# Expert additions written straight into an output with spare rows, and statistics, roots, counting products and gate waits moved

## The chip, the cores and the metric

The kernel runs on one core of a Trainium2 chip. The metric is the device time of one execution in microseconds (us), the median of three runs. For each version one further execution is recorded by the hardware profiler, and all rows below come from that one. The engines are TensorE (PE in the rows: matmuls, and PEld: its weight loads), VectorE (DVE), ScalarE (ACT) and GpSimd (POOL); SP only issues DMAs, and ACT and POOL issue some too. "SPq", "ACTq" are those engines issuing a DMA.

## The reference, cut to what matters

Two sequences of 1024 tokens, 256 features, all in fp32. Three sublayers, each added to the stream `x` after a layernorm:

```python
x = x + attn(layernorm(x))          # linear attention: q,k,v projections, elu+1, two decayed
                                    # running sums over time, normalised, times w_out
x = x + xattn(layernorm(x), ctx)    # 16 heads over 154 context rows:
    att = softmax(where(mask, -inf, (q @ k.T) / 8 * side))
    out = (att @ v) @ Wo + bo
x = x + ffn(layernorm(x))           # 8 experts, 2 per token, and a shared expert
    scores = softmax(x @ gate_w.T);  idx = top_k(scores + gate_b, 2)
    y = sum over the two chosen experts of score * (silu((x@w1+b1) * (x@w3+b3)) @ w2 + b2)
    z = shared expert of the same form
return x + y + z
```

## The kernel before, in words

Each engine runs a list of instructions written by hand; semaphores (`wait_ge`, `then_inc`) couple them. PSUM has eight banks, handed out in turn by the class `Banks`: every product of TensorE takes the next bank, and TensorE waits until the engine that reads the bank's last content has freed it (a pair that two matmul groups share is freed by one read). So the place of a product in TensorE's list decides which later product waits for the one who reads it.

Stage 1 (to about 105 us) is the linear attention in four chunks of 512 tokens. Stage 2 (to about 420 us) is the cross attention over 16 tiles of 128 tokens, in eight passes `u8` of two tiles `t0`, `t1`. In pass `u8` TensorE makes the scores of the pass (`scores`, L488), the queries of the next one (L471), transposes the softmax weights of the pass before (`weights_turned`, L521), multiplies them with the values in two halves (`product(u8, 0)` and `product(u8, 1)`, L537 and L541) and applies Wo (`combined`, L571; by halves L583). Around that VectorE multiplies scores with the side input (L1103), masks (L1114), takes maxima (L1121), sums' reciprocals (`total`, L1133) and adds the products' results (L1145, L1155); ScalarE does the exponentials (L819) and copies out of PSUM (L831, L754); GpSimd scales the weights (`scale`, L1496 and L1498). Layernorms go through `stats` (VectorE, L981 and L983, two instructions a tile), `rooting` (GpSimd, L1477 to L1482: the power -0.5), `normalise` (ScalarE L764, for two of them half on VectorE, L993) and `turned` (TensorE transposes, L367). `NORMS` names the twelve layernorms as (sublayer, chunk).

The gate of a chunk is `gate` (TensorE L502, then L511 transposed back; VectorE some twenty short steps at L1159, with `logits` L1164 before). `place(c)` counts for each token which row of its expert's list it gets: two small products (L594, L595) and VectorE's steps, of which L1210 frees the bank. GpSimd then scatters the normalised tokens twice into the DRAM buffer `xs` (`scatter_rows`, L1502), first with the first choice's weight and then with the second's (`second_weights`, L1508). The shared expert fills TensorE's list in between (`shared_mm` L606, `shared_out` L618; VectorE `shared_act` L1234 and L1246 to L1259; GpSimd `add_sb2` L1527).

Stage 3 (from about 420 us) are 39 tiles of 128 rows of `xs`, each for one expert: read (SP, L1672), transposed (L689), two products (L700), transposed (L710), last product (L720), and the result, times the token's weight, is added to the output rows by an indirect DMA of GpSimd (L1583) that adds in DRAM. These additions go to `zs`, an internal DRAM tensor of 3968 rows: 2048 for the tokens and 1920 spare ones on which the padding rows land. `zs` is first filled with `x` plus the shared expert (`base`, L1665). After the last two additions SP and ScalarE each copy half of the first 2048 rows of `zs` to the output:

```python
            e.dma_start(outr[half:N, :], zs[half:N, :]).then_inc(to_out, 16)   # ScalarE, L963
            e.dma_start(outr[0:half, :], zs[0:half, :]).then_inc(to_out, 16)   # SP, L1729
```

An addition `s` waits for the addition `s-2`, and for `s-1` where tile `s` begins another expert.

Of the kernel before, what the change touches and what calls it, by code (L numbers as in the profile page):

```python
# [15 lines left out]
P = 128  # L16
# [144 lines left out]
def decoder(nc, A, xs, zs, out):  # L161
    with ExitStack() as ctx:
# [139 lines left out]
        base_zs = sem("base_zs")  # L302
        base_zs3 = sem("base_zs3")
        to_zs = [sem(f"to_zs{i}") for i in range(2)]
        to_out = sem("to_out")
# [48 lines left out]
        def _(e):  # L354
# [191 lines left out]
            def values(u8, between, amid=None):  # L546
# [104 lines left out]
            for u8 in range(1, NU):  # L651
# [13 lines left out]
                combined(u8 - 1)  # L665
# [10 lines left out]
            shared_out(3, 0)  # L676
# [47 lines left out]
            rows_turned(0)  # L724
            for s in range(NS + 2):
# [16 lines left out]
        def _(e):  # L742
            w = Waits(e)

            def turned(k, c):
# [5 lines left out]
                for h in range(2):  # L751
# [207 lines left out]
            half = N // 2  # L959
            outr = out.rearrange("b s d -> (b s) d")  # L960
            for s in (NS - 2, NS - 1):
                e.wait_ge(to_zs[s % 2], added(s))
            e.dma_start(outr[half:N, :], zs[half:N, :]).then_inc(to_out, 16)  # L963
            e.wait_ge(to_out, 32)

        @block.vector
        def _(e):
# [198 lines left out]
            def gate(c, amid=None):  # L1166
# [3 lines left out]
                w.wait_ge(to_xs, 128 * c)  # L1170
# [9 lines left out]
                step(e.tensor_tensor, ga[:, :, :], lg[:, :, :], per_expert(gbB[:, :]), ALU.add)  # L1180
                for i, ox in enumerate((o1, o2)):
# [80 lines left out]
            normalise(1, 0)  # L1262
            stats(1, 1)
# [30 lines left out]
            for u8 in range(1, NU):  # L1294
                t0, t1 = 2 * u8, 2 * u8 + 1
                gating = (u8 - 3) // 2 if u8 >= 3 and u8 % 2 else None
                scores(t0)
# [38 lines left out]
                if u8 < 7:  # L1336
                    attended(u8 - 1)
            for hf in range(2):
# [15 lines left out]
            stats(3, 3, 0, 2)  # L1354
# [76 lines left out]
            def results(s):  # L1431
                u = bank["y", s]
                w.wait_ge(full[u.i], u.filled)
                if s >= 4:
                    w.wait_ge(to_zs[s % 2], added(s - 4))
# [21 lines left out]
        def _(e):  # L1457
# [53 lines left out]
            def scatter(c, between=None):  # L1511
                w.wait_ge(placed.sem, placed[c])
                for i in range(4):
# [283 lines left out]
```

## Time and profile before

| | us |
|---|---|
| median of 3 runs | 605.5 (605.31 to 607.53) |
| the profiled execution's own time | 605.35 |
| its span | 603.5 |
| TensorE busy | 569.9 |
| VectorE, ScalarE, GpSimd busy | 437.6, 311.7, 234.3 |

The span is what the profiler's records cover; 1.85 us of the profiled execution's own time lie around it. The granted TensorE clock was full (1.00, the upper of its levels) in every stretch with work in it up to 588 us. In the timeline rows the first number is the start, the second the length; brackets hold the idle time of that engine just before, and who ended it.

### The profile page before, as it was taken

The page shows a single profiled execution, that of the slowest core. Times are in us where ns is not written, and L with a number is a line of the kernel's source. Part 1 is how long each engine was busy: PE and PEld are TensorE (multiplying, and loading weights), DVE is VectorE, ACT ScalarE, POOL GpSimd, SP SyncE. Part 2 cuts the span into 40 slices and gives each one's busy share as a digit, 9 for nine tenths or more (in the row PEclk, how much of TensorE's full clock was granted, in tenths as well). Part 3 has the DMA queues.
Part 4 walks back from the last instruction along what each step waited for, and adds up shares of the span by engine and source line. Part 5 has one row for each costly group of instructions (what it writes and reads, how often), then busy time and mean ns, then how long its engine had stood idle before and what let it go on. Part 6 is the DMA issues. An engine that isn't in the chain of part 4 may idle for free.

```text
span 603.5 us, 11032 instructions
## 1 busy us (share of the span) xinstructions
PE 569.9 (94%) x3625; PEld 434.0 (72%) x3625; DVE 437.6 (73%) x817; ACT 311.7 (52%) x985; POOL 234.3 (39%) x227
## 2 busy tenths in 40 slices
PE   4999999999999999999999999999999999999990
PEld 2546657787788878688787868777777777777770
DVE  3999999999686979749697498566575555555550
ACT  2642424388869794877959569424233232322320
POOL 2010010227453745367342684262354334333341
PEclk9999999999999999999999999999999999999996
DMA  9910004246250502415133149764544343443425
GB/s 305 364 46 2 1 1 167 87 166 236 106 207 5 194 18 93 153 35 211 36 115 123 45 146 304 240 247 121 136 96 71 57 68 62 62 71 54 63 28 163
DMA packets 36647, 71.00 MB, mean 118 GB/s; under 512 B 5184, under 2 KB 29472, under 8 KB 34080
## 3 DMA queue, kind: packets, MB, share of 16 engines
q1 hardware_dynamic: 28272, 59.18, 29.7%
q0 software_dynamic: 7152, 9.34, 9.3%
q10 hardware_dynamic: 1168, 1.78, 0.9%
q8 instruction: 30, 0.49, 0.3%
q14 instruction: 25, 0.20, 0.1%
HBM read 58.86 MB, written 17.48 MB: 126 GB/s over the span
## 4 chain that ended last, share of the span: by engine, by line
PE 35%; DVE 23%; issue 17%; DMA 14%; POOL 5%; ACT 2%; POOLq 2%; DVEq 0%; SPq 0%
DMA zs_dram<-R 13%; PE pb L571 7%; DVE R L1035 6%; PE pb L471 6%; PE pb L521 4%; PE pb L606 4%; PE pb L488 4%; PE pb L537 4%; DVE R L1058 3%; PE pb L618 2%; DVE R L1013 2%; DVE mx L1121 1%; POOLq L1573 1%; PE pb L541 1%; DMA xs_dram<-xn,pos 1%
## 5 line engine op out<-in xcount | busy, mean ns | idle before, releaser
L819 ACT ACTIVATE R<-R,mx 128x154 f32<-128x154 f32 x256 | 104.3, 414 | 0.0
L700 PE MATMUL pb<-R 128*128 x312 | 98.8, 460 | 0.3 <-ACT R L932 0.3
L1583 POOL DMA_INDIRECT zs_dram<-R x39 | 60.6, 1553 | 96.2 <-DMA zs_dram<-R 51.0
L936 ACT ACTIVATE R<-R 128x352 f32<-128x352 f32 x39 | 19.4, 497 | 116.7 <-DVE R L1429 110.8
L700 PEld LDWEIGHTS pb<-R 128*128 128x128 f32 x312 | 56.2, 190 | 25.4 <-issue 0.6
L471 PE MATMUL pb<-xnT,wq 128*128 128x256 f32 x256 | 58.0, 383 | 0.0
L720 PE MATMUL pb<-R 128*128 (+1 forms) x234 | 57.0, 380 | 0.0
L810 ACT ACTIVATE R<-pb,bq 128x256 f32<-128x256 f32 x64 | 30.0, 473 | 49.7 <-PE pb L471 49.7
L471 PEld LDWEIGHTS pb<-xnT,wq 128*128 128x128 f32 x256 | 47.8, 190 | 7.8 <-issue 1.2
L1502 POOL DMA_INDIRECT xs_dram<-xn,pos x32 | 31.9, 997 | 52.4 <-DVE pos L1217 44.0
L571 PE MATMUL pb<-wo,R 128*128 128x256 f32 x224 | 50.0, 380 | 0.6 <-DVE R L1145 0.6
L1477 POOL TENSOR_TENSOR sd<-mv,cst 128x4 f32<-128x4 f32 x12 | 12.2, 1020 | 98.6 <-DVE mv L983 98.5
L831 ACT COPY R<-pb 128x512 f32<-128x512 f32 x80 | 40.8, 616 | 16.8 <-PE pb L521 16.8
L819 ACT ACTIVATION_READ_ACCUMULATOR R<-R,mx 128x1 f32 x256 | 49.1, 192 | 0.0
L1103 DVE TENSOR_TENSOR R<-pb,R 128x924 f32<-128x924 f32 (+1 forms) x48 | 45.2, 998 | 4.3 <-PE pb L488 3.3
L571 PEld LDWEIGHTS pb<-wo,R 128*128 128x128 f32 x224 | 42.3, 190 | 7.6 <-DVE R L1145 1.0
L1114 DVE SCALAR_TENSOR_TENSOR R<-R 128x2464 f32<-128x2464 uint8 (+1 forms) x17 | 47.0, 2766 | 0.0
L720 PEld LDWEIGHTS pb<-R 128*128 128x128 f32 (+1 forms) x234 | 41.6, 191 | 4.3 <-issue 0.2
L1121 DVE TENSOR_REDUCE mx<-R 128x16 f32<-128x2464 f32 (+1 forms) x17 | 43.6, 2565 | 0.4
L412 PE MATMUL pb<-xnT,R 128*128 128x512 f32 x96 | 43.0, 599 | 0.7 <-issue 0.7
L606 PE MATMUL pb<-xnT,sw 128*128 128x256 f32 (+1 forms) x192 | 43.5, 381 | 0.0
L1421 DVE TENSOR_TENSOR R<-pb,KV 128x352 f32<-128x352 f32 x39 | 20.4, 524 | 26.5 <-PE pb L700 21.6
(168 smaller groups left out, 1114.6 us busy)
## 6 DMA issues: line engine op xcount, KB each, us to landing
R<-in_fside_dram SPq DMA_DIRECT2D x16, 1232.0 KB, 5.6
R<-in_L_ffn_w_dram SPq DMA_DIRECT2D x16, 352.0 KB
R<-xs_dram SPq DMA_DIRECT2D x39, 129.0 KB, 2.1
R<-in_mask_dram SPq DMA_DIRECT2D x16, 308.0 KB, 2.9
KV<-in_ebias_dram SPq DMA_DIRECT2D x2, 1440.0 KB
zs_dram<-x SPq DMA_DIRECT2D x4, 512.0 KB
R<-in_L_ffn_w_dram SPq DMA_DIRECT2D x8, 256.0 KB, 4.3
zs_dram<-in_x_dram SPq DMA_DIRECT2D x1, 1920.0 KB
```

Source lines behind the costliest of these rows:

```text
L412: ins = e.matmul(pb[:, u.i, :], wqkv[:, k, col * P:(col + 1) * P], xnT[:, r, k, :], start=(k == 0), stop=(k == 1))
L471: ins = e.matmul(pb[:, u.i, 0:256], wq[:, k, j * P:(j + 1) * P], xnT[:, r, k, cols], start=(k == 0), stop=(k == 1))
L571: ins = e.matmul(pb[:, u.i, 0:D], oT[:, j, q * P:(q + 1) * P], wo[:, j, :], start=(j == 0), stop=(j == 7))
L606: ins = e.matmul(pb[0:mw, u.i, q * 256:q * 256 + 256], wm[:, k, lo:lo + mw], xnT[:, r, k, cols], start=(k == 0), stop=(k == 1))
L700: ins = e.matmul(pb[:, u.i, 0:F], xsT[:, s % 2, k, :], ew13[:, bass.ds(w_reg[s] * 1408 + q * 704 + k * F, F)], start=(k == 0), stop=(k == 1))
L720: ins = e.matmul(pb[:, u.i, 0:D], sT[0:mw, s % 2, m, :], ew2[0:mw, bass.ds(w_reg[s] * 768 + m * D, D)], start=(m == 0), stop=(m == 2))
L819: ins = e.activation(att[t % 3][:, h, :], att[t % 3][:, h, :], ACT.Exp, bias=mx[:, a4, 1, h:h + 1], accum_out=mx[:, a4, 2, h:h + 1])
L831: e.copy(pT[:, hf, 2 * k:2 * k + 2, :], pb[:, u.i, :].rearrange("p (i q) -> p i q", i=2)).then_inc(free[u.i], 1)
L1103: e.tensor_tensor(att[t % 3][:, 2 * lo:2 * hi, :].rearrange("p (r h) k -> p r h k", r=2), pb[:, u.i:u.i + 2, 0:n * SK].rearrange("p r (h k ...
L1114: e.scalar_tensor_tensor(out=att[t % 3][:, lo:hi, :], in0=mk[:, s, lo:hi, :], scalar=-BIG, in1=att[t % 3][:, lo:hi, :], op0=ALU.mult, op1= ...
L1121: e.tensor_reduce(mx[:, a4, 0, lo:hi], att[t % 3][:, lo:hi, :], AX.X, ALU.max).then_inc(*topped.next((t, hs, 0)))
L1583: e.indirect_dma_start(out=zs, out_offset=bass.IndirectOffsetOnAxis(ap=xsl[:, s % NR, D:D + 1].bitcast(U32), axis=0), in_=sY[:, s % 4, :], ...
```

## The change

1. `zs` is gone. The output tensor now has 3968 rows itself; the fills (`base`), the padding fill and the 39 additions go to `out`, and the first 2048 rows are its result. Both copies at the end are gone; SP waits for the last two additions (and for the fills).
2. TensorE's `place(0)` and `place(1)`, in passes 4 and 6, stand behind `product(u8, 0)` and not ahead of it.
3. In pass 1 `combined(0)` becomes `combined_by_halves(0)`: both tiles' sums over the first four blocks of `oT`, then both over the last four.
4. `shared_out(3, 0)` on TensorE stands behind the first transposes of stage 3.
5. VectorE copies the second half of the very first `xnT`, which ScalarE did.
6. `stats`: in pass 1 `stats(2, 2)` is cut in two, the first half ahead of the scores of the second tile. In pass 7 the second half of `stats(3, 2)` stands ahead of all scores. The first half of `stats(3, 3)` stands ahead of the last products' additions.
7. `rooting(3, 2)` on GpSimd, in pass 7, stands ahead of `scale(13)` and not behind it.
8. The waits of the gate: `gate(c)` waited for all scatters of the chunks before it at its start. It now waits only for the chunk that used the same `xn` buffer (for c = 3: 256 instead of 384), and further on for `second_weights(c-1)`, since it overwrites `wsel`. GpSimd's scatters wait for the chunk before.
9. `shared_act` in passes 3 and 5 stands in the middle of the gate's steps.

```diff
-def decoder(nc, A, xs, zs, out):
+def decoder(nc, A, xs, out):
@@ TensorE
+                product(u8, 0)
                 if amid is not None:
                     amid()
-                product(u8, 0)
@@
-                combined(u8 - 1)
+                if u8 == 1:
+                    combined_by_halves(0)
+                else:
+                    combined(u8 - 1)
@@
             place(3)
-            shared_out(3, 0)
...
             rows_turned(0)
+            shared_out(3, 0)
@@ ScalarE
-                for h in range(2):
+                for h in range(1 if n == 0 else 2):
...
-            for s in (NS - 2, NS - 1):
-                e.wait_ge(to_zs[s % 2], added(s))
-            e.dma_start(outr[half:N, :], zs[half:N, :]).then_inc(to_out, 16)
-            e.wait_ge(to_out, 32)
@@ VectorE
-                w.wait_ge(to_xs, 128 * c)
+                w.wait_ge(to_xs, 128 * sum(kc[0] == 3 for kc in NORMS[:NORMS.index((3, c)) - 1]))
...
+                if c:
+                    w.wait_ge(second.sem, second[c - 1])
...
             normalise(1, 0)
+            u = bank["xnT", 1, 0, 1]
+            w.wait_ge(full[u.i], u.filled)
+            e.tensor_copy(xnT[:, SLOT[1, 0], 1, :], pb[:, u.i, :]).then_inc(free[u.i], 1)
...
+                if u8 == 7:
+                    stats(3, 2, 2, 4)
                 scores(t0)
...
+                    stats(2, 2, 0, 2)
                     scores(t1, range(0, 2))
                     total(1)
                     scores(t1, range(2, 3))
-                    stats(2, 2)
+                    stats(2, 2, 2, 4)
...
-                if gating is not None:
+                if gating is not None and u8 < 7:
                     stats(3, gating, 2, 4)
...
-                    gate(gating, amid_gate if u8 == 7 else None)
-                if u8 in FILL:
+                    gate(gating, amid_gate if u8 == 7 else lambda: shared_act(*FILL[u8]))
+                elif u8 in FILL:
                     shared_act(*FILL[u8])
...
+            stats(3, 3, 0, 2)
             for hf in range(2):
                 product(7, hf)
             place(2)
...
-            stats(3, 3, 0, 2)
             for q in range(2):
                 attended(7, (q,))
@@ GpSimd
+                if u8 == 7:
+                    rooting(3, 2)
                 scale(2 * u8 - 1)
...
-                if u8 > 2 and u8 in BETWEEN:
+                if 2 < u8 < 7 and u8 in BETWEEN:
                     rooting(*BETWEEN[u8])
...
                 e.indirect_dma_start(
-                    out=zs, out_offset=bass.IndirectOffsetOnAxis(ap=xsl[:, s % NR, D:D + 1].bitcast(U32), axis=0),
-                    in_=sY[:, s % 4, :], in_offset=None, compute_op=ALU.add).then_inc(to_zs[s % 2], 16)
+                    out=out, out_offset=bass.IndirectOffsetOnAxis(ap=xsl[:, s % NR, D:D + 1].bitcast(U32), axis=0),
+                    in_=sY[:, s % 4, :], in_offset=None, compute_op=ALU.add).then_inc(to_out[s % 2], 16)
@@ SP
+            w.wait_ge(base_out, 64)
+            w.wait_ge(base_out3, 16)
             for s in (NS - 2, NS - 1):
-                w.wait_ge(to_zs[s % 2], added(s))
-            e.dma_start(outr[0:half, :], zs[0:half, :]).then_inc(to_out, 16)
+                w.wait_ge(to_out[s % 2], added(s))
@@ host
-    out = nc.dram_tensor("out_0_dram", (B, S, D), F32, kind="ExternalOutput").ap()
+    out = nc.dram_tensor("out_0_dram", (ZROWS, D), F32, kind="ExternalOutput").ap()
-    return r.results[0]["out_0_dram"]
+    return r.results[0]["out_0_dram"][0:N].reshape(B, S, D)
```

The order on TensorE in pass 6 before, around the counting product (`gt` with `R` and `ones`; `ident` rows are transposes of weights, `R,KV` rows the product with the values):

```order
L521 MATMUL pb<-ident,R 128x128
L594 MATMUL pb<-gt,R 128x32
L595 MATMUL pb<-gt,ones 128x32
L537 MATMUL pb<-R,KV 64x256 x8
L541 MATMUL pb<-R,KV 64x256 x8
L521 MATMUL pb<-ident,KV 128x128
```

and of the change:

```order
L520 MATMUL pb<-ident,R 128x128
L536 MATMUL pb<-R,KV 64x256 x8
L540 MATMUL pb<-R,KV 64x256 x8
L593 MATMUL pb<-gt,R 128x32
L594 MATMUL pb<-gt,ones 128x32
L520 MATMUL pb<-ident,KV 128x128
```

The two counting matmuls have moved behind the first half's product, so the bank they take lies four places later in the turn.

The order on VectorE at the start of pass 7 before (from the last Wo result of pass 6 to the first mask):

```order
L1155 TENSOR_TENSOR x<-pb,x 128x256 x2
L1103 TENSOR_TENSOR R<-pb,R 128x924 x2
L1103 TENSOR_TENSOR R<-pb,R 128x616
L1133 RECIPROCAL mx<-mx 128x16
L1103 TENSOR_TENSOR R<-pb,R 128x924 x2
L1103 TENSOR_TENSOR R<-pb,R 128x616
L981 BN_STATS st<-x 128x6
L983 BN_AGGR mv<-st 128x2
L981 BN_STATS st<-x 128x6
L983 BN_AGGR mv<-st 128x2
L1259 TENSOR_TENSOR x<-pb,x 128x256 x2
L1114 SCALAR_TENSOR_TENSOR R<-R 128x2464
```

and of the change:

```order
L1150 TENSOR_TENSOR x<-pb,x 128x256 x2
L976 BN_STATS st<-x 128x6
L978 BN_AGGR mv<-st 128x2
L976 BN_STATS st<-x 128x6
L978 BN_AGGR mv<-st 128x2
L1098 TENSOR_TENSOR R<-pb,R 128x924 x2
L1098 TENSOR_TENSOR R<-pb,R 128x616
L1128 RECIPROCAL mx<-mx 128x16
L1098 TENSOR_TENSOR R<-pb,R 128x924 x2
L1098 TENSOR_TENSOR R<-pb,R 128x616
L1256 TENSOR_TENSOR x<-pb,x 128x256 x2
L1109 SCALAR_TENSOR_TENSOR R<-R 128x2464
```

The four statistics instructions have moved from between the scores and the mask to ahead of the scores.

The order on GpSimd in pass 7 before (`scale(13)`, then `rooting(3, 2)`, then `add_sb2(2)`):

```order
L1496 TENSOR_TENSOR R<-R,mx 128x8x26
L1498 TENSOR_TENSOR R<-R,mx 128x1024
L1496 TENSOR_TENSOR R<-R,mx 128x8x26
L1498 TENSOR_TENSOR R<-R,mx 128x1024
L1477 TENSOR_TENSOR sd<-mv,cst 128x4
L1478 TENSOR_TENSOR nm<-mv,cst 128x4
L1480 TENSOR_TENSOR rs<-sd,cst 128x4
L1482 TENSOR_TENSOR nm<-nm,rs 128x4
L1527 TENSOR_TENSOR x<-x,R 128x256 x4
```

and of the change:

```order
L1480 TENSOR_TENSOR sd<-mv,cst 128x4
L1481 TENSOR_TENSOR nm<-mv,cst 128x4
L1483 TENSOR_TENSOR rs<-sd,cst 128x4
L1485 TENSOR_TENSOR nm<-nm,rs 128x4
L1499 TENSOR_TENSOR R<-R,mx 128x8x26
L1501 TENSOR_TENSOR R<-R,mx 128x1024
L1499 TENSOR_TENSOR R<-R,mx 128x8x26
L1501 TENSOR_TENSOR R<-R,mx 128x1024
L1531 TENSOR_TENSOR x<-x,R 128x256 x4
```

The root's four short instructions now come before the four of `scale(13)`.

## Rows read from the trace of the kernel before

**Rows 1.** The page: busy time; then the additions' group (busy, mean ns, idle before).

```profile
PE 569.9 (94%) x3625; PEld 434.0 (72%) x3625; DVE 437.6 (73%) x817; ACT 311.7 (52%) x985; POOL 234.3 (39%) x227
...
L1583 POOL DMA_INDIRECT zs_dram<-R x39 | 60.6, 1553 | 96.2 <-DMA zs_dram<-R 51.0
```

**Rows 2.** Waits of TensorE: us in total, times, longest us.

```profile
PE pb L367 <- ACT xn L764: 2.4, 3, 1.1
...
PE pb L537 <- DVE ga L1210: 1.1, 1, 1.1
PE pb L594 <- DVE gt L1197: 1.0, 1, 1.0
PE pb L521 <- POOL R L1498: 0.9, 1, 0.9
...
PE pb L571 <- DVE R L1145: 0.6, 1, 0.6
PE pb L700 <- ACT R L932: 0.3, 1, 0.3
```

**Rows 3.** Timeline of the end; its last stretch, busy us of PE, PEld, DVE, ACT, POOL.

```profile
590.54 1.55 POOL L1583 DMA_INDIRECT zs_dram<-R  x1 [0.65 <-issue]
...
594.41 0.60 ACTq L963 DMA_DIRECT2D out_dram<-zs_dram  x1
...
594.40:603.50 9.10, 0.00 (x0) 0.00 (x0) 0.00 (x0) 0.00 (x0) 0.00 (x0) 0.50 0.63 230
```

**Rows 4.** DMA issues: size, median us from issue to landing.

```profile
out_dram<-zs_dram ACTq DMA_DIRECT2D x1, 8.7
```

**Rows 5.** Busy view of two stretches, columns as above.

```profile
160.00:228.00 68.00, 68.00 (x548) 56.34 (x547) 52.58 (x79) 57.42 (x209) 36.45 (x35) 1.00 0.27 94
...
420.00:588.00 168.00, 167.41 (x753) 123.56 (x752) 96.39 (x220) 47.58 (x159) 66.04 (x46) 1.00 0.41 73
```

**Rows 6.** Timeline of pass 1.

```profile
137.79 2.15 DVE L1103 TENSOR_TENSOR R<-pb,R 128x924 f32<-128x924 f32 x2 [1.01 <-issue]
...
143.15 4.38 POOL L1498 TENSOR_TENSOR R<-R,mx 128x1024 f32<-128x1024 f32 x1
```

**Rows 7.** Timeline of pass 4: the mask and GpSimd's scaling at once.

```profile
274.94 3.71 DVE L1114 SCALAR_TENSOR_TENSOR R<-R 128x2464 f32<-128x2464 uint8 x1
276.02 2.68 POOL L1477 TENSOR_TENSOR sd<-mv,cst 128x4 f32<-128x4 f32 x1
```

**Rows 8.** Timeline of pass 4: TensorE behind the counting product.

```profile
249.01 0.66 PE L367 MATMUL pb<-ident,xn 128*128 128x128 f32 x4 [1.20 <-DVE ga L1210]
```

**Rows 9.** Timeline of pass 7.

```profile
343.83 2.85 DVE L1103 TENSOR_TENSOR R<-pb,R 128x924 f32<-128x924 f32 x3 [0.72 <-PE pb L488]
...
349.46 0.42 DVE L981 BATCH_NORM_STATS2 st<-x 128x6 f32<-128x256 f32 x1
...
350.54 0.72 DVE L1259 TENSOR_TENSOR x<-pb,x 128x256 f32<-128x256 f32 x2
...
351.18 3.07 DVE L1114 SCALAR_TENSOR_TENSOR R<-R 128x2464 f32<-128x2464 uint8 x1
351.63 2.68 POOL L1477 TENSOR_TENSOR sd<-mv,cst 128x4 f32<-128x4 f32 x1
...
357.91 1.09 PE L367 MATMUL pb<-ident,xn 128*128 128x128 f32 x8 [1.06 <-ACT xn L764]
...
365.54 0.28 DVE L1164 COPY gl<-pb 128x128 f32<-128x128 f32 x1
```

**Rows 10.** Timeline from the last layernorm to the last gate.

```profile
402.12 1.09 PE L367 MATMUL pb<-ident,xn 128*128 128x128 f32 x8 [1.14 <-ACT xn L764]
...
406.84 0.27 PE L511 MATMUL pb<-ident,gl 128*128 128x128 f32 x1
...
407.41 2.76 POOL L1527 TENSOR_TENSOR x<-x,R 128x256 f32<-128x256 f32 x4
409.65 0.56 DVE L1171 COPY xn<-tokid 128x4 int32<-128x4 int32 x1 [3.98 <-DMA xs_dram<-xn,pos]
```

More of the change, by code:

```diff
@@ L301, in decoder @@
         pad_xs = sem("pad_xs")
[L302 to L305, printed above, removed]
+        base_out = sem("base_out")
+        base_out3 = sem("base_out3")
+        to_out = [sem(f"to_out{i}") for i in range(2)]
         zeroed = signal("zeroed", ["ones", "cnt", "pad0", "pad1"])
@@ L957, in _ @@
                     hidden_turned(s - 1)
-            half = N // 2
-            outr = out.rearrange("b s d -> (b s) d")
-            for s in (NS - 2, NS - 1):
-                e.wait_ge(to_zs[s % 2], added(s))
-            e.dma_start(outr[half:N, :], zs[half:N, :]).then_inc(to_out, 16)
-            e.wait_ge(to_out, 32)
         @block.vector
@@ L1512, in scatter @@
                 w.wait_ge(placed.sem, placed[c])
+                w.wait_ge(to_xs, 128 * c)
                 for i in range(4):
@@ L1557, in _ @@
             w.wait_ge(placed.sem, placed[2])
+            w.wait_ge(to_xs, 128 * 2)
             for i in range(4):
@@ L1565, in _ @@
             w.wait_ge(placed.sem, placed[3])
+            w.wait_ge(to_xs, 128 * 3)
             for i in range(4):
@@ L1664, in base @@
                 w.wait_ge(free[d.i], d.drained)
-                e.dma_start(zs[c * CT:c * CT + CT, :].rearrange("(t p) d -> p t d", p=P),
+                e.dma_start(out[c * CT:c * CT + CT, :].rearrange("(t p) d -> p t d", p=P),
                             x[:, 4 * c:4 * c + 4, :]).then_inc(to, 16)
@@ L1669, in read @@
                 if s >= NR:
-                    w.wait_ge(to_zs[s % 2], added(s - NR))
+                    w.wait_ge(to_out[s % 2], added(s - NR))
                 v = e.value_load(sei[0:1, 1, s:s + 1], min_val=0, max_val=XROWS - P)
@@ L1680, in _ @@
                 if t == 4:
-                    e.dma_start(zs[N:ZROWS, :], A["x"].rearrange("b s d -> (b s) d")[0:ZROWS - N, :]
-                                ).then_inc(base_zs, 16)
+                    e.dma_start(out[N:ZROWS, :], A["x"].rearrange("b s d -> (b s) d")[0:ZROWS - N, :]
+                                ).then_inc(base_out, 16)
                 if t == 13:
-                    base(0, base_zs)
+                    base(0, base_out)
             for r in range(2):
@@ L1692, in _ @@
             fetch_w2()
-            base(1, base_zs)
+            base(1, base_out)
             fetch_eb(0, 3)
@@ L1710, in _ @@
                 read(s)
-            base(2, base_zs)
+            base(2, base_out)
             w.wait_ge(prows.sem, prows[0])
@@ L1715, in _ @@
                 e.dma_start(xs[bass.ds(v, P), :], A["pad"][ex * P:(ex + 1) * P, :]).then_inc(pad_xs, 16)
-            base(3, base_zs3)
+            base(3, base_out3)
             for s in range(NR, NA):
@@ L1723, in _ @@
                 read(s)
-            half = N // 2
-            outr = out.rearrange("b s d -> (b s) d")
+            w.wait_ge(base_out, 64)
+            w.wait_ge(base_out3, 16)
             for s in (NS - 2, NS - 1):
-                w.wait_ge(to_zs[s % 2], added(s))
-            e.dma_start(outr[0:half, :], zs[0:half, :]).then_inc(to_out, 16)
+                w.wait_ge(to_out[s % 2], added(s))
 def layout(inputs):
@@ L1790 @@
         aps[name] = nc.dram_tensor(f"in_{name}_dram", a.shape, mybir.dt.from_np(a.dtype), kind="ExternalInput").ap()
-    out = nc.dram_tensor("out_0_dram", (B, S, D), F32, kind="ExternalOutput").ap()
+    out = nc.dram_tensor("out_0_dram", (ZROWS, D), F32, kind="ExternalOutput").ap()
     xs = nc.dram_tensor("xs_dram", (XROWS, XW), F32, kind="Internal").ap()
-    zs = nc.dram_tensor("zs_dram", (ZROWS, D), F32, kind="Internal").ap()
-    decoder(nc, aps, xs, zs, out)
+    decoder(nc, aps, xs, out)
     r = _run(nc, [arrays], core_ids=[0])
-    return r.results[0]["out_0_dram"]
+    return r.results[0]["out_0_dram"][0:N].reshape(B, S, D)
```

10 lines of the change are left out of this document (4 added, 6 removed).

## The prediction, made before the changed kernel was run

> **What bounds the kernel now.** I read the busy shares first: TensorE is busy 94% of the span [rows 1]. Then its waits, which are short and few [rows 2]: apart from its start it almost never stands still for more than 1.2 us. From this the reader is to take the method: a microsecond is gained only where TensorE's stream stands still, or ahead of and behind it. Then the end of the timeline: the last addition is issued at 590.54, it has landed when the copy out is issued at 594.41, and from 594.40 to 603.50 no engine is busy at all [rows 3]; the copy that ScalarE issues lands after 8.7 us [rows 4]. So 9.1 us at the end are pure copy.
>
> In stage 3 the additions could be a second bound: GpSimd is idle 96.2 us ahead of them, of which 51.0 us end with an earlier addition's landing [rows 1]. But the other 45 us end with something else, mostly VectorE's result, so that the chain of additions catches up with TensorE again and again, and TensorE is busy 167.4 of the 168 us from 420 to 588 [rows 5].
>
> **The change part by part.** The sum is made against the profiled execution's own 605.35 us (span 603.50 and 1.85 around it), 0.15 below the median of the runs.
>
> *The copies.* Without them the program ends when SP sees the last addition landed, at the 594.41 of before. Between the copy's landing (594.41 + 8.7 = 603.1) and the span's end lie 0.4 us, which I leave in: the new end would be 594.7. Term: -8.8, bounds -9.1 and -8.4 (something like 0.4 more of closing work).
>
> *The counting products (item 2).* In pass 4 TensorE's second transposes wait 1.20 us [rows 8] for VectorE to read the counting product's bank, since that bank comes round eight takings later; in pass 6 it is the value product that waits 1.1 us [rows 2]. Behind `product(u8, 0)` the counting product takes a bank four places later. I followed the turn of the banks through the code: in pass 4 it comes round again only at the last pair of `product(3, 1)`, about 2 us after the point where TensorE waited, and in pass 6 only after the whole of it. VectorE does its part no later than now (it waits for the same product ahead of it in both cases, and that product even comes a little earlier). Both waits go: -2.25, bounds 0 (if ScalarE's copies hold TensorE at the same point) and -2.3.
>
> *Wo by halves in pass 1 (item 3).* L571 waits 0.6 us for the second half's addition [rows 2], with a quarter of its work done. By halves, half of its work is free of that wait, and that is longer than the wait: -0.6.
>
> *Statistics in pass 1 (item 6).* VectorE is idle 1.01 us ahead of the scores of the second tile [rows 6] (it waits for GpSimd's scaling), and the first two tiles' statistics cost 1.08 (as 349.46 to 350.54 in [rows 9]), so they lie in idle time and the mask L1114 comes some 1.0 us earlier, at 141.9. But there GpSimd is in its scaling. Rows 7 show what happens then: the mask, asked for at 274.94 in the middle of a scaling that ends at 276.0, took 3.71 us where one alone takes 2.7, and GpSimd's next instruction, 0.2 us elsewhere, took 2.68: each waits until the other's instruction is over. In pass 1 now it is GpSimd that loses 2.5 us (L1498: 4.38 [rows 6]), and TensorE waits 0.9 us for it [rows 2]. With an earlier mask GpSimd's short instruction at 142.7 is caught and not the long one behind it, and the end of its scaling comes at about 147.8 in place of 147.53: +0.3 on TensorE, bounds +0.6 and -0.9 (if it comes free of the mask).
>
> *Pass 7 (items 6 and 7).* TensorE waits 1.06 us for ScalarE's normalised rows [rows 9], which wait for the root on GpSimd, which stood behind `scale(13)` and then, for 2.68 us, behind a mask [rows 9]. With the statistics first (1.08 us, of which 0.72 lie in VectorE's idle time at 343.1) and the root in GpSimd's idle time, ScalarE can start when its own copies are done, about 1.4 us earlier: that wait goes. But VectorE is the one that is late in this pass. Its scores come 0.36 to 0.42 later, so does the reciprocal on which `scale(13)` waits, and GpSimd's last long instruction runs from 350.2 to 352.1. The mask, asked for at 350.65 (earlier than 351.18, since the statistics are out of its way), meets that instruction as in [rows 7] and can begin only at 352.1: it ends at 354.8 and not 354.25. All of VectorE's chain behind it is 0.55 late: the addition L1145, whose bank `product(6, 1)` needs, and the gate's copy L1164 (365.54), for which TensorE's L511 waits already. So the 1.06 us come back there, with 0.6 on top: +0.6, bounds -1.06 (the root's delay alone counts) and +0.9.
>
> The page "SBUF — State Buffer" of the Trainium skill, section "SBUF: two separate sides", has it as an exclusive lock: a VectorE instruction with two SBUF inputs and a GpSimd instruction that reads SBUF take it for the whole instruction, and the other blocks fully. Rows 7 agree. By a rule of shared bandwidth instead, an overlap would only stretch both in proportion, and pass 7 would come out nearer to -1.0 than to +0.6.
>
> *The last layernorm (item 6).* TensorE waits 1.14 at 402.12 [rows 10]. The statistics of its first half now lie in VectorE's wait for the last value products, and the root comes 0.5 us earlier. But VectorE has its own half to normalise, behind a chain of steps that begins with TensorE's shared output and is not moved, and it ends 0.2 us before the wait does. So 0.2 is gained, not 0.5: -0.2.
>
> *The last gate (items 4 and 8).* VectorE stands 3.98 us waiting for scatters at 409.65 [rows 10]. It would be able to go on once L511 is done (406.84 + 0.27). GpSimd's four additions from 407.41 to 410.17 [rows 10] will catch some four of its steps, so that about half of the 3 us is lost again, and the end of the gate moves from 416.5 to about 415. That is enough: TensorE's fill L606 lasts until then, and the wait of 1.0 at L594 goes. With the first rows of stage 3 transposed ahead of `shared_out(3, 0)`, ScalarE's copy is hidden under it: the 0.3 ahead of L700 goes too. -1.35, bounds 0 and -1.4. The new wait for `second_weights(2)` is met (GpSimd does it at 402, as soon as four scatters have landed), and nothing queues behind it. The scatters' new waits on GpSimd are for transfers long landed.
>
> *At nothing:* the copy by VectorE (item 5), since it waits for TensorE's transposes just as ScalarE's second copy did, and VectorE is idle there; if it were in the way, it would cost its 0.7. `shared_act` amid the gate (item 9): VectorE's total up to the next scores stays as it is. Bounds for both together -0.3 and +0.7.
>
> Sum: -8.8 - 2.25 - 0.6 + 0.3 + 0.6 - 0.2 - 1.35 = -12.3. From 605.35: **593.0 us**.
>
> **The rivals.**
> (a) *Waits return.* TensorE's waits are ends of loops over VectorE, ScalarE and GpSimd; take one away, and the next link is late. For it: two waits on ScalarE's rows add to 2.4 [rows 2], right where slack is small. Against: from 160 to 228 us TensorE is busy all of the 68 us [rows 5], so the loops have slack. If only the copies go: 605.35 - 8.8 = 596.5.
> (b) *No collision in pass 7.* The mask falls where GpSimd has ended, or the lock costs it nothing. Then 1.06 is won, not 0.6 lost, and the 0.3 in pass 1 does not come: 593.0 - 1.7 - 0.3 = 591.0.
> (c) *Additions into the output tensor are slower, and the kernel is slower.* One addition now takes 594.41 - 590.54 = 3.9 us from issue to landing. Two can be under way, so that a pair of tiles may take 3.9 + 0.7 (landing to next issue) before the chain of additions binds, and TensorE gives a tile every 4.3 us (168 us from 420 to 588 [rows 5], 39 tiles), 8.6 a pair. The landing must grow beyond 7.9 us before it decides. To be 3 us above 605.35, 15.3 us would have to be lost over some 19 pairs, 0.8 each: a landing of 8.7 us, 608.4 in all. Against it: the copy wrote 1 MB on each of two queues into the output in 8.7 us [rows 4], so the output is no slow target.
> (d) *It doesn't do what it says:* closing the program with a larger output costs as much as the copy did. Then only the waits count: 605.35 - 3.5 = 601.9.
>
> **How the numbers follow.** Forecast 0.55, its own range 591.5 to 595. (a) 0.20, (b) 0.18, (c) 0.03, (d) 0.04. For 8 in 10 the range reaches over (b) and (a), with the bounds of the unknown terms: 589.8 to 597.3. A measurement of this kernel tells about 0.5% from no change, 3 us: below 602.5 is faster. All of the forecast, (a), (b) and most of (d): faster 0.95; same 0.02 (the rest of (d)); slower 0.03, which is (c).
>
> **What would show it.** No DMA from the output to itself at the end; the last event about 4 us after the last addition's issue. TensorE's waits on L1207 (L1210 before) gone, and on the Wo rows of pass 1. In pass 7 no wait at L367 but one of 0.5 or more at the value product and at L510 (L511 before), and a mask of 4 us beside a scaling: that would show the collision; a mask of 2.7 and no wait at L510 would show (b). At the last gate no 4 us wait on VectorE, and no wait at L593. Wrong I would be if the step from issue to landing of the additions were other than 3.9 us, or if the waits named in (a) stood at the same places with other names.

## The result, and the profile after

| | before | after |
|---|---|---|
| median of 4 runs each, us | 605.4 (605.29 to 607.53) | 596.68 (595.4 to 598.15) |
| the profiled execution's own time | 605.35 | 597.44 |
| its span | 603.5 | 595.6 |
| last addition issued | 590.54 | 587.97 |

The ratio after to before is 0.985, with an interval of 0.9821 to 0.9878. So the change is worth 8.7 us of median. The forecast was 593.0, with a range of 589.8 to 597.3: the range holds the result, but the forecast's own range without its rivals, 591.5 to 595, does not, and the profiled execution ends 4.4 us later than the sum of steps said. Single executions of one kernel lie 2 to 5 us apart; one cause of that is found below.

The profile's page of after, to be held against [rows 1]: busy time first, then the group of the additions (busy, mean ns, idle before).

```profile
PE 570.6 (96%) x3625; PEld 435.1 (73%) x3625; DVE 441.6 (74%) x818; ACT 311.1 (52%) x984; POOL 231.7 (39%) x227
...
L1591 POOL DMA_INDIRECT out_dram<-R x39 | 60.6, 1553 | 96.4 <-DMA out_dram<-R 63.1
```

TensorE's waits (us in total, times, longest), against [rows 2]:

```profile
PE pb L536 <- DVE R L1140: 1.5, 1, 1.5
PE pb L366 <- DVE xn L988: 1.1, 1, 1.1
PE pb L510 <- DVE gl L1159: 1.0, 1, 1.0
...
PE pb L520 <- POOL R L1501: 0.8, 1, 0.8
```

The reader sees that the waits for the counting product's bank, for the Wo rows and for the last counting product are gone, and that two stand in pass 7: 1.5 us at the value product (L536), where before had none, and 1.0 at the transposed gate (L510), where before had 0.2. Of the two waits of 1.1 us for normalised rows, the one in pass 7 is gone. The one of the last layernorm stands where it stood, under another name: VectorE's half (L988) now ends it, and not ScalarE's.

Where the time went shows best if both traces are cut at the same instructions of TensorE (first weight load of a pass's scores, of a transposed gate, and so on; the end is the start of the last closing entry, 0.05 us ahead of the span's end). Lengths in us:

| stretch | before | after | difference | forecast |
|---|---|---|---|---|
| start to the first denominators (L441, L440 after) | 35.34 | 37.17 | +1.83 | 0 |
| from there to the scores of pass 1 | 97.35 | 97.34 | 0 | 0 |
| pass 1 | 30.47 | 29.36 | -1.11 | -0.3 |
| passes 2, 3 and 5, each | 28.99, 34.85, 37.65 | the same | 0 | 0 |
| pass 4 | 39.97 | 38.52 | -1.45 | -1.15 |
| pass 6 | 37.95 | 36.76 | -1.19 | -1.1 |
| pass 7 to its transposed gate | 23.31 | 24.71 | +1.40 | +0.6 |
| to the last transposed gate | 40.75 | 40.70 | -0.05 | -0.2 |
| from there to the last addition's issue | 183.91 | 181.92 | -1.99 | -1.35 |
| last addition's issue to the end | 12.95 | 7.60 | -5.35 | -8.8 |

The differences add to -7.9, the difference of the two profiled executions. Without the start, which differs from one execution to the next (see e3), they are 9.7 us apart. In every later trace the untouched stretches behind the start come out within 0.03 us of these numbers (the passes) or within some 0.3 (the others), so that this table measures single parts of the change far better than whole times do.

**The end.** The last rows of the timeline of after, then the busy view of what is left (length, busy us of PE, PEld, DVE, ACT, POOL, granted clock, DMA share, GB/s), against [rows 3]:

```profile
587.97 1.55 POOL L1591 DMA_INDIRECT out_dram<-R  x1 [0.59 <-issue]
...
592.00:595.60 3.60, 0.00 (x0) 0.00 (x0) 0.00 (x0) 0.00 (x0) 0.00 (x0) 0.50 0.00 0
```

For 3.6 us neither an engine nor a DMA works. What runs is found by asking for L162, the line that closes the program on every engine. Its rows give queue, operation, count, duration in ns (least, median, longest) and first and last start. GpSimd's is the same in before (first fence) and in after (second) but for its start:

```profile
L162 POOLq DRAIN  x1: 7646/7646/7646, 590.3 to 590.3; - x1
```

```profile
L162 POOLq DRAIN  x1: 7646/7646/7646, 587.7 to 587.7; - x1
...
L162 SPq DRAIN  x1: 7/7/7, 592.0 to 592.0; - x1
```

GpSimd closes with a drain of 7.65 us. In before it was over at 598.0, beneath the copies; in after it ends at 595.4 and is the last thing that happens, 3.4 us behind SP.

**The start.** TensorE's weight loads of the first projections, in before and then in after:

```profile
13.35 0.19 PEld L412 LDWEIGHTS pb<-xnT,R 128*128 128x128 f32 x1 [0.24 <-issue]
13.77 0.19 PEld L412 LDWEIGHTS pb<-xnT,R 128*128 128x128 f32 x1 [0.24 <-issue]
```

```profile
13.86 0.34 PEld L411 LDWEIGHTS pb<-xnT,R 128*128 128x128 f32 x1 [0.52 <-issue]
14.71 0.34 PEld L411 LDWEIGHTS pb<-xnT,R 128*128 128x128 f32 x1 [0.52 <-issue]
...
17.03 0.19 PEld L411 LDWEIGHTS pb<-xnT,R 128*128 128x128 f32 x1 [0.28 <-issue]
```

In after TensorE's loads take 0.34 us and step by 0.85 up to 17 us, where before has 0.19 and 0.43, and everything behind is 1.8 us late. The traces' own clock records begin at 12.1 us in before and at 16.8 in after, each with the upper level. The profile's column of the granted clock prints 1.00 also where there is no record yet, so its 1.00 says nothing of the time ahead of these points. In before too the weight loads at 8.22 and 8.74 us take 0.34. So "full in every stretch" holds for before only from 12.1 us on, and the slow start is a clock that rises 4.7 us later.

**Pass 7.** Timeline of after:

```profile
348.31 1.90 POOL L1501 TENSOR_TENSOR R<-R,mx 128x1024 f32<-128x1024 f32 x1
348.67 4.12 DVE L1109 SCALAR_TENSOR_TENSOR R<-R 128x2464 f32<-128x2464 uint8 x1
...
354.75 2.78 POOL L1531 TENSOR_TENSOR x<-x,R 128x256 f32<-128x256 f32 x4 [4.55 <-ACT xn L766]
355.58 0.63 DVE L1119 TENSOR_SCALAR mx<-mx 128x16 f32<-128x16 f32 x1
356.24 0.65 DVE L1122 SCALAR_TENSOR_TENSOR mx<-mx 128x16 f32<-128x16 f32 x1
...
357.54 1.95 PE L536 MATMUL pb<-R,KV 128*64 128x256 f32 x16 [1.47 <-DVE R L1140]
```

The mask (L1109) is caught by the scaling as forecast (4.12 us). What the forecast had not seen is the second collision: GpSimd's bias additions (L1531) now start earlier, at 354.75 and not 357.93, and VectorE's two small steps (L1119, L1122) take 0.63 and 0.65 us where they take 0.17 each in before. The Trainium skill ("SBUF — State Buffer", section "SBUF: two separate sides") says that whichever of the two engines starts first has the shared port for its whole instruction, and the other blocks. These rows agree: each step ends with a bias addition, and four additions take 2.78 us, 0.7 each.

### The profile page after: what moved, and what is told of

Read it like the earlier page. It is cut to its first block, busy times and chain, and to the rows that moved or that the text cites. A ratio compares the mean times of both kernels' runs of the same rounds, so it can differ in the third digit from the quotient of the medians.

```text
span 595.6 us, 11035 instructions
## 1 busy us (share of the span) xinstructions
PE 570.6 (96%) x3625; PEld 435.1 (73%) x3625; DVE 441.6 (74%) x818; ACT 311.1 (52%) x984; POOL 231.7 (39%) x227
## 4 chain that ended last, share of the span: by engine, by line
PE 49%; DVE 21%; issue 12%; DMA 9%; POOL 4%; ACT 2%; POOLq 1%; SPq 0%; DVEq 0%
DMA out_dram<-R 8%; PE pb L701 7%; DVE R L1030 6%; PE pb L470 6%; PE pb L570 6%; PE pb L605 6%; PE pb L520 5%; PE pb L536 4%; PE pb L487 4%; PE pb L721 3%; DVE R L1053 3%; PE pb L617 2%; DVE R L1008 2%; PE pb L540 1%; DVE R L1072 1%
## 5 line engine op out<-in xcount | busy, mean ns | idle before, releaser
L1591 POOL DMA_INDIRECT out_dram<-R x39 | 60.6, 1553 | 96.4 <-DMA out_dram<-R 63.1
L1480 POOL TENSOR_TENSOR sd<-mv,cst 128x4 f32<-128x4 f32 x12 | 9.8, 815 | 99.9 <-DVE mv L978 99.8
L1109 DVE SCALAR_TENSOR_TENSOR R<-R 128x2464 f32<-128x2464 uint8 (+1 forms) x17 | 48.6, 2861 | 0.0
L411 PE MATMUL pb<-xnT,R 128*128 128x512 f32 x96 | 45.0, 622 | 0.8 <-issue 0.8
L570 PE MATMUL pb<-wo,R 128*128 128x256 f32 x192 | 42.5, 380 | 0.0
L570 PEld LDWEIGHTS pb<-wo,R 128*128 128x128 f32 x192 | 36.4, 190 | 5.4 <-issue 0.4
L605 PEld LDWEIGHTS pb<-xnT,sw 128*128 128x128 f32 (+1 forms) x192 | 34.2, 181 | 7.0 <-issue 0.8
```

The lines of the kernel that those rows point to most:

```text
L411: ins = e.matmul(pb[:, u.i, :], wqkv[:, k, col * P:(col + 1) * P], xnT[:, r, k, :], start=(k == 0), stop=(k == 1))
L570: ins = e.matmul(pb[:, u.i, 0:D], oT[:, j, q * P:(q + 1) * P], wo[:, j, :], start=(j == 0), stop=(j == 7))
L605: ins = e.matmul(pb[0:mw, u.i, q * 256:q * 256 + 256], wm[:, k, lo:lo + mw], xnT[:, r, k, cols], start=(k == 0), stop=(k == 1))
L1109: e.scalar_tensor_tensor(out=att[t % 3][:, lo:hi, :], in0=mk[:, s, lo:hi, :], scalar=-BIG, in1=att[t % 3][:, lo:hi, :], op0=ALU.mult, op1= ...
L1591: e.indirect_dma_start(out=out, out_offset=bass.IndirectOffsetOnAxis(ap=xsl[:, s % NR, D:D + 1].bitcast(U32), axis=0), in_=sY[:, s % 4, :] ...
```

## The experiments

The theory after the comparison: the end is bound by GpSimd's drain (A), the slow start falls by chance and not by part 5 (C), and pass 7 pays a second collision (E). Each ratio is to executions of before timed beside it, whose median was 606.65 us for the e kernels, 606.28 for the f ones and 605.8 for the g ones.

**e1_no_pool_drain**

```diff
-        block = ctx.enter_context(nc.Block())
+        block = ctx.enter_context(nc.Block(no_gpsimd_drain=True))
```

> The kernel after, but the block that holds all engines' programs ends without GpSimd's own drain. In the trace of after GpSimd's last queue entry is a drain of 7.65 us that begins at 587.74; SP has seen the last addition land at 591.8, and the span ends at 595.62, 0.2 behind the drain. Theory A, the drain sets the end: the end falls to about 592.0, so -3.6 us against after (596.7 to about 593.1), and the last event stands some 4.1 us behind the last addition's issue, which is what the prediction said. Theory B, closing after an addition into the output takes its 3.6 us by itself, and the drain only waits alongside: no change (596.7).

Measured: 593.97 (591.9 to 594.22), ratio 0.9785 (0.9764 to 0.9806). Its profiled execution has the slow start too, and its span is 592.3 against 595.6; from the last addition's issue to the end it takes 4.34 us and not 7.60. Theory A holds, B falls.

**e2_copies_only**: before, with part 1 alone (the diff above without anything else).

> The kernel before with part 1 of the change alone: additions and fills go into the output with spare rows, no copies at the end. Prediction as it stands: -8.8 against before, 596.6. Theory A (GpSimd's drain of 7.65 us, which ended at 597.96 in before under the copies, is now what ends last): 590.31 + 7.65 + 0.2 = 598.2 in place of 603.5 of span, -5.3: 600.1. Rival (closing with a larger output costs as much as the copies): 605.4.

Measured: 600.93 (599.27 to 602.03) beside 606.65 of before, ratio 0.991 (0.9892 to 0.9928). Last stretch 7.60, as in after; all others as in before (the additions' stretch 0.23 less, the rest within 0.05, but the start: 34.89). So part 1 is worth 5.4 us, not 8.8; the rival (closing costs as much as the copies) falls.

**g2_wait_then_drain**: after, with its drain, and at GpSimd's end

```diff
+            for s in (NS - 2, NS - 1):
+                w.wait_ge(to_out[s % 2], added(s))
```

> The kernel after with its closing drain, but GpSimd waits for the last two additions to land before it ends. The drain took 7.65 us in three traces, always begun 0.22 ahead of the last addition, and lay 3.5 us behind its landing. Theory H, its length is a fixed piece of work that starts when GpSimd's last instruction is over (5.9 us behind the end of the last addition, 1.55 long): the end moves to the landing + 5.9, 9.9 us or more behind the last addition's issue in place of 7.6, so 2.3 us slower in the span. Theory I, it waits for the landing and then does some 3.5 us of its own: no change, 7.6. Theory J, most of it is passed in parallel with the landing whatever the order: the drain is short and the end comes earlier, some 4.3.

Measured: 598.69 (one run), 10.06 us from the last issue to the end. The drain is shorter by just the 1.55 and 0.22 us of the last addition:

```profile
L162 POOLq DRAIN  x1: 5867/5867/5867, 590.8 to 590.8; - x1
```

Theory H: 5.87 us of fixed work that begins when GpSimd's last instruction is over, whether its transfers have landed or not. I and J fall.

**e3_scalar_copies_both**

```diff
-                for h in range(1 if n == 0 else 2):
+                for h in range(2):
...
-            e.tensor_copy(xnT[:, SLOT[1, 0], 1, :], pb[:, u.i, :]).then_inc(free[u.i], 1)
```

> The kernel after with part 5 undone: ScalarE copies both halves of the first xnT. In the trace of after TensorE's first projections (from 12.87) step by 0.85 us each until 16.9 and then by 0.43; in that of before they step by 0.43 from 13.35 on. That puts everything behind it 1.8 us later. Theory C, it falls differently from one execution to the next whatever the copy: executions of this kernel spread over some 2 us as those of after do (595.4 to 598.2), the median stays at 596.7 within 0.5. Theory D, VectorE's copy brings it about: every execution is 1.8 us faster, 594.9, with a spread under 0.6.

Measured: 595.06, and one by one 594.98, 595.02, 595.06, 597.24, 597.54: two groups some 2.3 apart, as in after (595.4, 595.92; 597.44, 598.15). The profiled one is of the lower group, and its weight loads take 0.19 from 12.83 on. That the upper group has the slow start is likely by its distance, but none of it was profiled. What makes D fall are g2 and g3 below: both have part 5, and both start quickly (their clock records begin at 12.1 and 11.8 us):

```profile
13.43 0.19 PEld L411 LDWEIGHTS pb<-xnT,R 128*128 128x128 f32 x1 [0.24 <-issue]
```

This row is of g3. So part 5 doesn't bring the slow start by itself. That it makes it no likelier rests on the upper groups of e3 and of before (607.53) alone: the three traces without it (before, e2, e3) all start quickly. The lower groups of e3 and after differ by 0.4 us, which so few executions don't tell from nothing.

**e4_busy_from_start**

```diff
+            w.wait_ge(zeroed.sem, zeroed["ones"])
+            for _ in range(28):
+                e.matmul(pb[:, 7, 0:P], ones[:, :], ones[:, :], start=True, stop=True)
             keys(0, 1)
```

> The kernel after with 28 matmuls of 128 columns on a tile of ones put at TensorE's start, into a bank that is overwritten later; they do no useful work and fill TensorE's first 7.2 us, in which it waits for the first weights. Theory C (the slow step of the first projections belongs to TensorE having had little work before, and its moment shifts from one execution to the next): the projections step by 0.43 from the start in every execution, the spread over executions falls below 0.8, the fastest are at or below the fastest of after (595.4), the median about 595.0. Theory D (it has to do with the copy of VectorE, or the data): no change, 596.7, spread 2 or more. If the added matmuls run into the first keys product (7.23), up to 1 us is lost.

Measured: 595.18; five executions between 594.75 and 595.5, one at 598.96. The profiled one has the quick start. As C has it, but for the one far out, which the forecast of a spread below 0.8 did not allow and which was not profiled.

**f0_both**: e1's and e4's edits together, with 19 matmuls.

> The kernel after without GpSimd's closing drain and with 19 matmuls of 128 columns on ones ahead of TensorE's first work (they do nothing useful). In the run with 28 of them the added work took 7.86 us from 0.99 and ran 1.65 us over the arrival of the first weights (7.23), so 19 should end at about 7.2. Expected: 597.44 - 3.3 (the drain, span 595.6 against 592.3 at the same slow start) - 2.4 (last addition issued at 585.5 and not 587.95 when the first projections step by 0.43) = 591.7, nearly all executions within 0.8. It is also the base of the next three. Rival (the drain's 3.3 and the start's 2.4 hide in one another): 593.9.

Measured: 591.75, ratio 0.9768 (0.9742 to 0.9795). The median is as expected, the spread (591.14 to 595.85) is not. The profiled execution is the slowest of the five. Busy view of TensorE in f0_both and then in e4_busy_from_start (length, PE busy, granted clock, DMA share, GB/s):

```profile
6.00:9.00 3.00, 1.77 (x14) 1.00 1.02 357
9.00:12.00 3.00, 0.80 (x4) 0.93 1.07 381
12.00:15.00 3.00, 2.06 (x9) 0.50 1.09 358
15.00:18.00 3.00, 3.00 (x4) 0.50 1.04 393
```

```profile
6.00:9.00 3.00, 3.00 (x29) 1.00 1.05 368
9.00:12.00 3.00, 2.15 (x13) 1.00 1.07 371
12.00:15.00 3.00, 2.94 (x7) 1.00 1.09 355
15.00:18.00 3.00, 3.00 (x8) 1.00 1.04 389
```

**f1_pass7_undone**: f0 with parts 6 and 7 undone in pass 7.

```diff
-                if u8 == 7:
-                    stats(3, 2, 2, 4)
                 scores(t0)
...
-                if gating is not None and u8 < 7:
+                if gating is not None:
                     stats(3, gating, 2, 4)
...
-                if u8 == 7:
-                    rooting(3, 2)
                 scale(2 * u8 - 1)
...
-                if 2 < u8 < 7 and u8 in BETWEEN:
+                if u8 > 2 and u8 in BETWEEN:
                     rooting(*BETWEEN[u8])
```

> The base (closing drain off, TensorE busy from the start) with the moves of pass 7 undone: second half of stats(3, 2) and rooting(3, 2) at their places of before. The prediction had these moves at +0.6, so -0.6 here, 591.1. What the trace of after shows is larger: its lead over before shrinks from 1.65 us at the last transposes of pass 7 (354.11 against 355.76) to 0.53 at the transposed gate (365.35 against 365.88): -1.1, 590.6, with a wait of 1.06 for the normalised rows back and the ones of 1.47 at the value product and 1.01 at the transposed gate gone. Rival (no collision, the moves won 1.06): 592.8.

Measured: 591.27, ratio 0.9742 (0.9722 to 0.9762). Pass 7 takes 23.30 us, -1.40; TensorE's only wait in it is the 1.1 for the normalised rows. The moves of pass 7 cost 1.4 us. The rival (no collision) falls.

**f2_bias_behind_mask**: f0, and in pass 7 on GpSimd

```diff
+                if u8 == 7:
+                    w.wait_ge(masked.sem, masked[NT - 1, (0, H)])
                 if gating:
                     add_sb2((u8 - 3) // 2)
```

> The base with the moves of pass 7 kept, but GpSimd's four additions of the bias (L1531, 2.78 us from 354.75 in after) wait for VectorE's second mask of the pass. In after they begin while VectorE is in its small steps L1119 and L1122, which take 0.63 and 0.65 us instead of 0.17 each (before had them at 357.93, behind those steps). Theory E: this second collision is the part that the prediction missed; without it VectorE's addition L1140 and all behind it come 0.9 us earlier, TensorE's wait at the value product falls from 1.5 to about 0.6, and that at the transposed gate to about 0.1: -0.9, 590.8. Rival: the additions collide with the maximum or the sums behind the mask instead, or TensorE waits for another bank: 591.7.

Measured: 590.74, ratio 0.9741 (0.9723 to 0.9759). Pass 7 takes 23.78, -0.92; the small steps take 0.17 again, the wait at the value product is 0.5. The wait at the transposed gate stays at 1.0, not 0.1: TensorE is there 0.9 earlier too. Theory E holds: 0.92 of the 1.40 is the second collision. The 0.48 left over is what the forecast had at 0.6.

**f3_counting_ahead**: f0 with part 2 undone.

> The base with part 2 undone: the counting products of passes 4 and 6 ahead of product(u8, 0) again. The prediction gave this part 2.25 us: 593.9, with waits of TensorE for L1207 of 1.2 and 1.1 us back. Rival (the time comes back later in the passes, as in other loops): at most half of it, 592.8 or less.

Measured: 595.53, ratio 0.9814 (0.9793 to 0.9835). Pass 4 takes 39.85 (+1.34), pass 6 37.95 (+1.19), and both waits for the bank are back (1.2 and 1.0). Part 2 is worth 2.53 us, and none of it comes back later: passes 5 and 7 and the stretches behind keep their length.

**g1_wo_not_halved**: e1 with `combined(u8 - 1)` for pass 1 too.

> The kernel after without GpSimd's closing drain, and with part 3 undone: pass 1 applies Wo tile by tile (combined), not by halves. What is read is the stretch from TensorE's first scores of pass 1 to those of pass 2: 30.47 us in before, 29.35 in after, so -1.12 where the prediction had -0.3 for parts 3 and 6 together (-0.6 and +0.3). Theory F, the halves are worth the wait of 0.6 and a further part that the profile of before did not show as a wait, and the statistics are worth nothing: 30.4 to 30.5. Theory G, the halves are worth 0.6 and the earlier statistics the rest: 29.95. By the prediction as it stands (statistics +0.3): 29.95 with the other 0.5 unexplained.

Measured: 594.36 (one run). Pass 1 takes 29.77 us: the halves are worth 0.41, and the other 0.70 is left for the statistics, the only other part that touches pass 1 (theory G, with a larger share for the statistics). Without the halves the wait for the Wo rows is only 0.15 and not 0.6:

```profile
159.15 1.13 PE L570 MATMUL pb<-wo,R 128*128 128x256 f32 x4 [0.15 <-DVE R L1137]
```

**g3_gate_waits_all**: e1 with VectorE's wait `w.wait_ge(to_xs, 128 * c)` back at the gate.

> The kernel after without the closing drain, and with the wait of part 8 put back: the gate's first step waits for all earlier scatters. Read is the stretch from the last transposed gate on TensorE to the first transposes of stage 3, and from there to the last addition: 13.08 and 170.83 in before (183.91), 9.21 and 172.71 in after (181.92), so -1.99 for parts 4 and 8; the prediction had -1.35. If the wait is what the gain comes from: 183.6 or so for the sum (0.3 for part 4), with a wait of VectorE of 3 to 4 us at the last gate and one of TensorE of 1 us or more at the last counting product. Rival (the order of the shared output gives it): 182.2 or less.

Measured: 593.75 (one run). The two stretches take 10.60 and 172.84, 183.44 in sum: some 1.5 us of the 2.0 are this wait (1.39 of it in the first stretch, the steadier one), and some 0.5 is left for part 4. The waits are back, VectorE's and TensorE's:

```profile
DVE xn L1166 <- DMA xs_dram<-xn,pos: 3.4, 1, 3.4
```

```profile
PE pb L593 <- DVE gt L1194: 1.1, 1, 1.1
```

**g4_sums_first**: the edits of f2, but with 28 matmuls and not 19, and in pass 7

```diff
                 if u8 == 7:
+                    total(t0 - 1)
                     stats(3, 2, 2, 4)
                 scores(t0)
                 if u8 > 1:
-                    total(t0 - 1)
+                    if u8 < 7:
+                        total(t0 - 1)
```

> An improved kernel: after, without the closing drain, with 28 matmuls of ones at TensorE's start, and in pass 7 GpSimd's bias additions behind VectorE's second mask, and the reciprocal of tile 13's sums ahead of the statistics and the first scores. With that GpSimd can scale tile 13 from about 343.1 instead of 344.33 (the root comes first), ends at about 347.9 instead of 349.1, and VectorE's mask waits 0.2 instead of 1.4 us for it. Pass 7 to the transposed gate takes 24.70 us in after, 23.31 in before, 23.78 with the bias additions moved alone. Theory: 22.6 to 22.9 here, and the execution with a quick start at 595.0 - 3.4 - 2.0 = 589.6; median below 590.2. Rival (the scores become late for TensorE or ScalarE by the reciprocal and statistics ahead of them, and give it back): 23.8 or more, 590.7 as with the bias additions alone.

Measured: 589.73 (589.11 to 590.88, 6 runs), ratio 0.9733 (0.9711 to 0.9754): the lowest median of the study. Its interval overlaps f2's; that it gains over f2 is shown by pass 7, which takes 22.46 against 23.78, 0.85 less than in before. GpSimd's last scaling and VectorE's mask, from its timeline, now hardly meet:

```profile
345.98 1.90 POOL L1506 TENSOR_TENSOR R<-R,mx 128x1024 f32<-128x1024 f32 x1
...
347.55 2.91 DVE L1112 SCALAR_TENSOR_TENSOR R<-R 128x2464 f32<-128x2464 uint8 x1
```

## Why the prediction was right, and where it was not

- **The copies: mis-sized, -8.8 against -5.35.** The reading that failed is "So 9.1 us at the end are pure copy", and with it the step "Between the copy's landing and the span's end lie 0.4 us, which I leave in: the new end would be 594.7". Its bounds (-9.1 to -8.4) came from what ended last, and the prediction did not ask which other work ended beneath the copies. GpSimd's drain did: e1 and g2 show that it ends 5.87 us after GpSimd has issued the last addition, and e2 that nothing else of part 1 counts. Rival (d), that closing costs as much as the copy, has a part of the truth: closing costs 3.4 us of it, but by the drain and not by the output's size. The sign "the last event about 4 us after the last addition's issue" failed in after (7.6) and came true in e1 (4.34).
- **The start, +1.8, was in no step.** It isn't part 5, which g2 and g3 have with a quick start, but the clock's rise, at 12.1 us in the profiled execution of before and at 16.8 in that of after.
- **Counting products: right.** -2.25 forecast, -2.53 by f3; the followed turn of the banks was the right view. Taking a wait away gave more than the wait printed: 1.34 and 1.19 for 1.2 and 1.0 here, 1.39 for 1.1 in g3, 0.41 for 0.15 in g1. The likely reason is that the profile models where a matmul ends: it gives each product of the Wo rows 0.38 us, while they follow each other every 0.22 us (24 in 5.45), so that a printed wait begins some 0.16 late. That is an estimate, and it covers only about half of the difference in g1 and g3.
- **Pass 1: right in the sign of the sum, wrong in its terms.** The halves gave 0.41 and not 0.6, because the statistics had already taken most of the same wait (0.62 in before, 0.15 in g1). -0.70 is left for the statistics, where +0.3 stood. The collision is there as described: GpSimd's short instruction takes 3.02 us. But its scaling ends at the same point of the pass as before, and TensorE's transposes wait for it 0.8 us as before (0.9), so the collision cost nothing. VectorE's chain of masks and maxima, though, is earlier, and the Wo rows hang on it. That gain had no term.
- **Pass 7: the mechanism right, the size not.** +0.6 forecast, +1.40 by f1. The forecast's collision (mask of 4 us beside a scaling, waits at the value product and at the transposed gate) is there, and cost 0.48. The missing 0.9 is the bias additions, which were let go earlier by the very rows that the change brought forward (f2).
- **Last layernorm:** -0.2 forecast, -0.05 found, with the wait of 1.1 as before, now ended by VectorE's half. By the prediction's own words a wait at its old place under another name would show it wrong and rival (a) right; here it did so in this one place. **Last gate:** -1.35 forecast, -1.99 found; the wait on scatters gave some 1.5 of it (g3), where 1.0 stood. GpSimd's additions did stretch three of VectorE's steps (to 0.72, 0.65 and 0.32 us, from 0.19), but VectorE is done at 414.15, ahead of the end of TensorE's fill at 415.0, so that this costs TensorE nothing.
- **At nothing:** parts 5 and 9. Passes 3 and 5 keep their length to 0.01 us, and from the first transposes to the first projections TensorE takes 2.77 us against 2.66, so part 5 cost about 0.1.
- **The additions** land 3.8 us after issue (3.9 in before), so rival (c) falls. Rival (a), 596.5, comes nearest to the measured median, yet for another reason: the waits did not return outside pass 7, where two new ones add to 2.5 us.

That the time fell into the range is thus partly luck. Against the forecast stand +3.45 for the end, +1.8 for the start, +0.8 in pass 7 and +0.15 at the layernorm; for it -0.8 in pass 1, -0.4 in the counting products and -0.6 at the last gate. That is the 4.4. The range was wide enough for it by its rivals, not by its terms: the sum's own range ended at 595.

## What to carry to other kernels

When the last step of a program is taken away, list everything on every queue that ends beneath it, closing instructions too: the gain is the distance to the second last, not the length of the step. When an engine's wait is removed, follow what that engine and those that waited for it release earlier, and look what that meets on VectorE and GpSimd. And cut both traces at the same instructions: here stretches compared to hundredths of a microsecond where whole times differed by two from one execution to the next.

## What the runs showed of the hardware that was not expected

- GpSimd's closing drain takes 5.87 us behind its last instruction, whether the last additions have landed (g2) or not (7.65 in after, of which 1.8 pass before that instruction is over). Without the drain the end comes 4.0 to 4.4 us after the last addition's issue, of which 3.8 are its landing. No run here shows the drain in a program whose GpSimd issues no DMA.
- The TensorE clock can fall back to its lower level within the first 20 us (f0: 1.00, 0.50, then 1.00), and while it is low the first projections step by 0.85 and not 0.43 us. The upper level began anywhere between 10.9 us (e3) and 17.5 (e1, g1) in the traces without added matmuls: at 10.9 to 12.1 us in five of them and at 16.8 to 17.5 in three, with nothing between.
- The column of the granted clock reads 1.00 in the first microseconds of a trace also where weight loads of 0.34 us show the lower level.
